# The last stage of a perceiver kernel: raw rows multiplied, mean and deviation put in later, mixing matrices in two alternating chains, half of the mixing on TensorE

## The reference

```
x = x + xattn(layernorm(x), ctx, ...)
x = x + attn(layernorm(x), Wq, Wk, Wv, Wo)
x = x + ffn(layernorm(x), W_res, W_pre, W_post, ...)

# ffn: 4 streams of 256 channels, per token
x_norm = x * rsqrt(mean(x * x) + 1.19e-07)
H_res  = sinkhorn(x_norm @ W_res.T + H_res_base)       # 4 x 4, 50 iterations, tau 0.1
H_pre  = softmax(x_norm @ W_pre.T + H_pre_base)        # 4
H_post = softmax(x_norm @ W_post.T + H_post_base)      # 4
H_res  = (1 - g) * I + g * H_res                       # g = sigmoid(gate)
y      = (sum over n of H_pre[n] * stream n) @ W_branch
out i  = sum over j of H_res[i, j] * stream j  +  H_post[i] * y
```

## Time and profile before

| | us |
|---|---|
| median of 3 runs | 1221.07 |
| lowest and highest run | 1219.29, 1223.58 |
| the profiled execution | 1221.3 |
| span of its trace | 1219.3 |
| PE busy | 1042.8 (86%) |
| DVE busy | 838.3 (69%) |
| ACT busy | 471.3 (39%) |
| POOL busy | 187.7 (15%) |

### The profile page before, as it was taken

How to read it: one execution, slowest core, us unless ns; L and a number is a source line. 1 busy time by engine, 2 the same in 40 slices (tenths; PEclk the granted TensorE clock), 3 DMA queues, 4 the chain that set the end, 5 groups by cost and what they waited for, 6 DMA issues and landing times.

```text
span 1219.3 us, 17027 instructions
## 1 busy us (share of the span) xinstructions
PE 1042.8 (86%) x6208; PEld 872.5 (72%) x6208; DVE 838.3 (69%) x1588; ACT 471.3 (39%) x945; POOL 187.7 (15%) x192
## 2 busy tenths in 40 slices
PE   3999999999999999999999999999989898941100
PEld 2888888888888878888888878888867677741000
DVE  5743437567778778667688766745658997348888
ACT  3422324354455465444454543413232333132300
POOL 0000000233333222332222200000000000127100
PEclk9999999999999999999999999999989999965555
DMA  9785757234443222444443148995470400000001
GB/s 219 150 182 132 168 118 165 66 94 101 102 99 66 64 52 55 99 101 102 102 102 68 31 87 173 215 242 103 87 121 18 63 10 14 1 1 0 0 0 69
DMA packets 161544, 111.07 MB, mean 91 GB/s; under 512 B 73144, under 2 KB 153656, under 8 KB 161488
## 3 DMA queue, kind: packets, MB, share of 16 engines
q1 hardware_dynamic: 160432, 109.29, 41.3%
q10 hardware_dynamic: 1056, 1.05, 0.4%
HBM read 90.91 MB, written 18.87 MB: 90 GB/s over the span
## 4 chain that ended last, share of the span: by engine, by line
PE 75%; DVE 18%; ACT 3%; issue 2%; DMA 1%; SPq 0%; DVEq 0%; POOL 0%; ACTq 0%
PE ps L511 27%; PE ps L457 27%; PE ps L796 7%; PE ps L443 5%; PE ps L522 4%; PE ps L539 3%; DVE xr L1790 2%; DVE wt L1257 2%; DVE small L1762 1%; DVE small L1768 1%; DMA raw<-in_L_xattn_q_proj_w 1%; DVE small L1770 1%; DVE small L1766 1%; DVE small L1773 1%; DVE small L1764 1%
## 5 line engine op out<-in xcount | busy, mean ns | idle before, releaser
L511 PE MATMUL ps<-wt,act 128*128 128x512 f32 x1536 | 389.2, 397 | 0.0
L457 PE MATMUL ps<-wt,act 128*128 128x512 f32 x1440 | 330.8, 392 | 10.8 <-DVE wt L1257 10.8
L457 PEld LDWEIGHTS ps<-wt,act 128*128 128x128 f32 x1440 | 271.1, 189 | 68.5 <-DVE act L1241 7.6
L511 PEld LDWEIGHTS ps<-wt,act 128*128 128x128 f32 x1536 | 276.0, 189 | 49.3
L1257 DVE TENSOR_TENSOR wt<-raw,wt 128x512 fp32r<-128x512 f32 x192 | 120.1, 683 | 86.1 <-ACT wt L899 86.1
L899 ACT ACTIVATE wt<-raw 128x512 fp32r<-128x512 f32 x192 | 106.4, 623 | 97.8 <-PE ps L457 52.1
L1249 DVE STREAM_TRANSPOSE raw<-raw 128x1024 f32<-128x1024 f32 x96 | 112.7, 1218 | 37.3 <-DMA raw<-in_L_xattn_o_proj_w 20.6
L1241 DVE TENSOR_TENSOR act<-ps,act 128x512 fp32r<-128x512 f32 x112 | 75.7, 683 | 86.2 <-ACT act L894 86.2
L1803 POOL TENSOR_TENSOR small<-small 128x4 f32<-128x4 f32 (+2 forms) x64 | 71.3, 1115 | 397.3 <-DVE small L1271 391.4
L796 PE MATMUL ps<-wt,act 128*128 128x512 f32 x480 | 124.7, 412 | 5.6 <-DVE spare L1569 5.1
L894 ACT ACTIVATE act<-ps 128x512 fp32r<-128x512 f32 x112 | 65.9, 596 | 121.9 <-PE ps L443 121.6
(11 more groups left out here) (126 smaller groups left out, 1045.4 us busy)
## 6 DMA issues: line engine op xcount, KB each, us to landing
xr<-in_ctx SPq DMA_DIRECT2D x64, 256.0 KB, 5.8
raw<-in_L_xattn_o_proj_w SPq DMA_DIRECT2D x32, 512.0 KB, 14.3
raw<-in_L_xattn_q_proj_w SPq DMA_DIRECT2D x30, 512.0 KB, 9.2
q_rows<-G SPq DMA_DIRECT2D x64, 128.0 KB, 3.5
xr<-q_rows SPq DMA_DIRECT2D x16, 512.0 KB
ot_hi<-spare SPq DMA_DIRECT2D x64, 128.0 KB, 2.6
act<-ot_hi SPq DMA_DIRECT2D x32, 256.0 KB, 9.4
raw<-in_L_xattn_k_proj_w SPq DMA_DIRECT2D x8, 512.0 KB, 9.6
```

Of the source, the lines that this page charges most:

```text
L457: mm = pe.matmul(banks[t], lhs(p == 2, c, t), wt[:, n_slot, int(p == 1), c, :], start=(acc_from and q == 0), stop=(acc_to and q == 3 * NC ...
L511: mm = pe.matmul(bank, src[int(p == 2)][:, c, kt * P:(kt + 1) * P], wt[:, slot, int(p == 1), c, :], start=(q == 0), stop=(q == 3 * NC - 1))
```

## The change

It touches only what follows the output projection's products (and, ahead of them, where the statistics of a first half are taken).

1. **Raw rows.** PE turns `xr` itself (`turn_rows`): a tile's first half within block 12 + t, its second half within block 13 + t, both at `at_11`; for tile 3 the second half comes after block 15. The product with the 24 weight columns (`logits` on PE) is of raw rows; a product of a matrix of ones with the weights (`s24`) gives the sums by which the mean is taken off. On DVE `logits(t)` is now two instructions: `s24` times minus the mean, added to the product, then times `rz`, plus the base. `rz` now comes from the variance, without ACT's square. The first half's statistics are taken at blocks 9 to 11 and after the loop (`first_stats3`), the rest behind the last add (`last_stats3`). Normalising is ACT's (`normalise_out`, 1024 columns a tile).
2. **Two chains.** Chain 0 is tiles 0 and 1, chain 1 tiles 2 and 3; each works on 32 numbers per partition, with semaphores of its own (`sk_step`, `sk_in`, `sk_out`). Chain 0 runs 4 iterations (`HEAD`) alone, the two then 20 together, an instruction of the one after an instruction of the other; then chain 1 runs 4 alone while ACT serves chain 0, chain 0 runs 4 while ACT serves chain 1, 21 run together, chain 0 finishes, and chain 1 runs its last 4. An epoch is 25 iterations, so there is one new centring instead of four. The first centring has no logarithms any more: the maxima are taken off, and the first row sums are used as factors.
3. **The branch.** ACT makes diagonal matrices (`dmix`, identity times a column of `h8`, 8 of 128 columns a tile). PE sums the four streams by them (`branch`, 8 matmuls of 128 columns), multiplies with `wb` (2 of 256), and puts x + y times `H_post` into PSUM (`base`, 2 of 512 and 4 of 256 columns a tile). For tiles 2 and 3 ACT copies this to `xr`; for tiles 0 and 1 it stays in PSUM.
4. **The mixing.** For tiles 0 and 1 ACT makes 32 diagonal matrices of the mixing factors (`dres`) after `finish(0)`, PE multiplies them with `z` (`mix`, 32 matmuls of 256 columns, each waiting for its matrix) on top of what lies in PSUM, and ACT copies out. Tiles 2 and 3 stay on DVE, 32 instructions as before; tile 3 is stored in two halves.
5. POOL keeps only the roots and a memset of the ones.

The core of the diff:

```diff
-ITERS, EPOCH = 50, 10
+ITERS, EPOCH, HEAD = 50, 25, 4
@@ PE
+                    elif b >= 12:
+                        if b >= 13:
+                            turn_rows(b - 13, 1)
+                        turn_rows(b - 12, 0)
...
                 if b >= 13:
-                    feed(b - 13)
-            feed(3)
+                    logits(b - 13)
+            turn_rows(3, 1)
+            logits(3)
             for t in range(NT):
...
+                branch(t)
+                base(t)
+            for t in range(2):
+                mix(t)
@@ PE, new
+            def mix(t):
+                for half in range(2):
+                    bank = ps[:, base_banks[t][half], :]
+                    for i in (2 * half, 2 * half + 1):
+                        for j in range(NSTR):
+                            pe.wait_ge(d_res, 16 * t + 4 * i + j + 1)
+                            mm = pe.matmul(bank[:, (i % 2) * CW:(i % 2 + 1) * CW], dres[t][:, 4 * i + j, :],
+                                           z[:, t, j * CW:(j + 1) * CW], start=False, stop=(i % 2 == 1 and j == NSTR - 1))
+                    mm.then_inc(mix_done, 1)
@@ ACT
+            exp_chain(1)
+            exp_chain(1)
+            normalise_out(3)
+            sc.wait_ge(h8_in, 1)
+            sc.activation(h8, h8, ACT.Exp).then_inc(h8_out, 1)
+            branch(0)
+            branch(1)
+            log_chain(0)
+            exp_chain(0)
+            log_chain(1)
+            exp_chain(1)
+            branch(2)
+            branch(3)
+            for t in range(2):
+                sc.wait_ge(h_ready, 1)
+                for n in range(16):
+                    sc.activation(dres[t][:, n, :], ident[:], ACT.Copy, scale=hres[:, 16 * t + n:16 * t + n + 1]
+                                  ).then_inc(d_res, 1)
@@ DVE
+            last_stats3(0)
+            last_stats3(1)
+            logits(0)
+            last_stats3(2)
+            logits(1)
+            centre_rows(0)
+            centre_cols(0)
+            last_stats3(3)
+            first_iteration3(0)
+            logits(2)
+            for _ in range(HEAD):
+                iterate((0,))
+            logits(3)
+            centre_rows(1)
...
+            centre_cols(1)
+            first_iteration3(1)
+            joint = EPOCH - 1 - HEAD
+            for k in range(joint):
+                iterate((0, 1), last=0 if k == joint - 1 else None)
...
+            for k in range(HEAD):
+                if k == HEAD // 2:
+                    recentre(0)
+                iterate((1,), last=1 if k == HEAD - 1 else None)
+            for k in range(HEAD):
+                if k == HEAD // 2:
+                    recentre(1)
+                iterate((0,), fresh=0 if k == 0 else None)
+            for k in range(ITERS - EPOCH - HEAD):
+                iterate((0, 1), fresh=1 if k == 0 else None)
+            finish(0)
+            for k in range(HEAD):
+                iterate((1,))
+            finish(1)
@@ SP
+            for t, half, signal, count in ((0, None, mix_out, 2), (2, None, out_ready, 1), (1, None, mix_out, 4),
+                                           (3, 0, out_ready, 2), (3, 1, out_ready, 3)):
```

More of the change, by code:

```diff
@@ L769, in turn_out2, with turn_rows @@
                 tr.then_inc(o2_turned, 1)
[L771 to L781, removed]
+            def turn_rows(t, half):
+                pe.wait_ge(acc_free, (57 if half else 53) + t)
+                if t == 0:
+                    pe.wait_ge(o2_lo, 8)
+                else:
+                    pe.wait_ge(f_ready, 2 * t - 1 + half)
+                for j in range(4):
+                    tr = pe.transpose(ps[:, 6 + half, j * P:(j + 1) * P],
+                                      xr[:, t, (4 * half + j) * P:(4 * half + j + 1) * P], ident[:])
+                tr.then_inc(f_done, 1)
@@ new lines, in base @@
+            def base(t):
+                pe.wait_ge(lg_read, 4)
+                if t == 3:
+                    pe.wait_ge(base_added, 1)
+                for half in range(2):
+                    bank = ps[:, base_banks[t][half], :]
+                    pe.matmul(bank, ident[:], xr[:, t, half * UW:(half + 1) * UW], start=True, stop=False)
+                    if half == 0:
+                        pe.wait_ge(y_read, t + 1)
+                    for i in (2 * half, 2 * half + 1):
+                        mm = pe.matmul(bank[:, (i % 2) * CW:(i % 2 + 1) * CW], dmix[t % 2][:, 4 + i, :], yb,
+                                       start=False, stop=(t >= 2 and i % 2 == 1))
+                mm.then_inc(base_done, 1)
@@ L1212, in _, with copy_rows @@
[L1212 to L1218, removed]
+            sc.activation(gts[:, 1:2], gts[:, 0:1], ACT.Exp, scale=-1.0).then_inc(gate_exp, 1)
+            def copy_rows(t, half):
+                sc.wait_ge(f_done, 2 * t + half + 1)
+                if half == 0 and t >= 2:
+                    sc.wait_ge(lg_done, t - 1)
+                sc.activation(xT[t % 2][:, 4 * half:4 * half + 4, :], four(ps[:, 6 + half, :]), ACT.Copy
+                              ).then_inc(f_ready, 1)
@@ L1221, in _ @@
+            for t in range(2):
+                for half in range(2):
+                    sc.wait_ge(mix_done, 2 * t + half + 1)
+                    sc.activation(xr[:, t, half * UW:(half + 1) * UW], ps[:, base_banks[t][half], :], ACT.Copy
+                                  ).then_inc(mix_out, 1)
         @block.vector
@@ new lines, in invert_cols, with iterate @@
+            def invert_cols(c, last=False):
+                stepped(c)
+                r = v.reciprocal(ub[c], ub[c])
+                if last:
+                    ask(c, r)
+                else:
+                    step(c, r)
+            def iterate(chains, fresh=None, last=None):
+                for c in chains:
+                    if c != fresh:
+                        stepped(c)
+                        step(c, v.tensor_tensor(rows4(of(tk, c)), rows4(of(Kx, c)), over_i(ub[c]), ALU.mult))
+                for c in chains:
+                    if c == fresh:
+                        answered(c)
+                    else:
+                        stepped(c)
+                    step(c, v.tensor_reduce(ua[c], rows3(of(Kx if c == fresh else tk, c)), AX, ALU.add))
+                for c in chains:
+                    stepped(c)
+                    step(c, v.reciprocal(ua[c], ua[c]))
+                scale_rows(chains)
+                for c in chains:
+                    invert_cols(c, c == last)
@@ new lines, in _ @@
+            finish(1)
+            settle()
+            for t, parts in ((2, ((0, 1, 2, 3),)), (3, ((0, 1), (2, 3)))):
+                v.wait_ge(base_added, t - 1)
+                for streams in parts:
+                    for j in range(NSTR):
+                        settle()
+                        for i in streams:
+                            c = 16 * t + 4 * i + j
+                            o = xr[:, t, i * CW:(i + 1) * CW]
+                            done(v.scalar_tensor_tensor(o, z[:, t, j * CW:(j + 1) * CW], hres[:, c:c + 1], o,
+                                                        ALU.mult, ALU.add),
+                                 out_ready if (i, j) == (streams[-1], NSTR - 1) else dv)
```

390 lines of the change are left out of this document (216 added, 174 removed).

## The result

The changed kernel takes 1180.21 us (median of 4 runs, 1178.49 to 1180.74), the kernel before 1221.93 us in the runs beside it (4 runs): ratio 0.9655, 95% interval 0.9638 to 0.9671, faster by 41.7 us. The profiled execution took 1179.86 us, its span is 1178.1. The forecast was 1181.6.

The account below looks back on a forecast made before the run. DVE's path after the last product was taken to bound the tail; its stretches summed to 1176.7, plus 3.1 and 2.0, less 0.2, gave 1181.6 us, 39.5 less than before. Range 1174 to 1196, own case 1174 to 1188 (0.62).

Parts of the forecast that it names:

- The bound: After the last product, the tail is a DVE path, so what happens in it can be priced by DVE's timeline.
- The joint iterations: 41 iterations of both chains on DVE, twelve instructions each: 1.40 us apiece, bounds 1.32 and 1.68.
- the rival in which they don't: DVE instructions don't overlap: a joint iteration takes 2.8 us, +57 us, 1239 in all; chance 0.06.
- both bounds meet: In a joint pair on DVE, issue (2 x 0.11) and the wait within a chain (0.19 + 0.033) both give 0.22 us.
- The rival of slow issue behind a wait: DVE starts behind a wait need 0.14 instead of 0.11: a joint iteration costs 1.68, +11.5 us, 1193; chance 0.13.
- The centrings: Between the joint stretches, one new centring covered by the other chain's four iterations: 12.0 us, to 1126.2, no wait at ACT.
- The last product: PE from block 12 on: the last product ends 1.0 us later, at 1073.4, bounds +0.5 and +2.0.
- The collisions with POOL: DVE's long multiplies in the iterations fall together with POOL's adding and weighing and disappear with them: 5.7 us on L1762.
- half-width instructions and early iterations: The rest of the gain, 8 us: half-width instructions and four of chain 0's iterations run before 1085.5.
- The mixing on PE: After finish(0), from 1156.6: some 4 matmuls at the lower clock, then 28 at 0.48 to 0.55; 17 to 19 us, to 1175.
- The rival of a clock that stays low: PE's clock stays low through the mixing, which lasts 30.7 us to 1187.3; end at 1193; chance 0.17.
- The end: After DVE's mixing at 1176.7: 3.1 us to the span's end and 2.0 outside it, 1181.8, less 0.2 for the median.

Follow-up runs that it names:

- the third chain: The changed kernel with six more vector instructions on 32 numbers in each of the 41 joint iterations, one behind each pair, on data nothing reads: 1193.48 us.
- the added additions: The changed kernel with eight additions of 1024 columns on POOL beside the first joint stretch, on data nothing reads: 1193.88 us.

## Why the prediction was right

**The bound.** The tail was DVE's and still is: the last entries of the chain are its mixing, and what was taken off DVE came off the time (the mixing of two tiles: 13.9 us on DVE, 14.0 in the time).

**The joint iterations** were the largest term: 1.40 forecast, 1.39 measured. The two close pairs of the trace before gave the right answer to whether neighbours overlap, and the rival in which they don't, with the rule of the Trainium skill (VectorE: DVE Perf Modes, "The DRAIN you can't avoid") behind it, is out: the second of a pair starts 0.12 after the first, while that one's record lasts 0.19. What the same section says beside it, that an operation which is not held starts earlier, agrees with this. One step of the working was wrong though it did no harm: "both bounds meet". With the third chain a start takes 0.095 on the mean, so issue asks for 0.19 a pair, and only the wait of 0.23 binds. The rival of slow issue behind a wait (0.14) is out by the same rows.

**The centrings.** 11.0 us (1114.13 to 1125.15) instead of 12.0. One of them on DVE, two additions between chain 1's reciprocal and its next multiply:

```profile
1116.67 0.20 DVE L1884 RECIPROCAL small<-small 128x8 f32<-128x8 f32 x1
1116.79 0.14 DVE L1917 TENSOR_TENSOR small<-small 128x32 f32<-128x32 f32 x1
1116.96 0.19 DVE L1919 TENSOR_TENSOR small<-small 128x32 f32<-128x32 f32 x1
1117.07 0.19 DVE L1895 TENSOR_TENSOR small<-small 128x32 f32<-128x32 f32 x1
```

The multiply starts 0.40 after the reciprocal instead of 0.24, so the additions of one chain cost 0.16 us and not the 0.5 taken: they stand in the other chain's wait. Chain 0's fresh matrix also needs no first multiply, which I had not counted. Chain 1's saves nothing, since chain 0's multiply keeps that turn; the second joint stretch takes 29.2 us, 21 x 1.39. No wait at ACT, as forecast.

**The last product** was the step most off: +1.0 forecast within +0.5 to +2.0, +1.84 measured, and that it lies within the bounds is luck. The sum was about the stretch from the start of block 12 to the last product's end, and this takes 30.8 us (1043.49 to 1074.27) against 31.1 before (1041.34 to 1072.43): -0.3, outside the bounds. The clock gave back its share: it stays at 1.00 there, where block 14 before took 6.9 us instead of 5.5. The work inside was mis-sized: summed by durations it was 9.5 us, from start to start the 28 transposes take 2.7 and the three small products 5.1, 7.8 in all against 7.4 before; on the other side a block that is cut in two takes 5.70 instead of 5.51, 0.7 in the four. What makes the +1.84 is that block 12 starts 2.15 us later (1043.49 against 1041.34), of which 1.0 is there by 907 us, where the code is the same. The other kernels here with this PE code have block 12's start between 1040.8 and 1046.3, each needs 30.8 us from there, and their last products end between 1071.6 and 1077.0. The start moves by itself, by more than the term is worth, and the 1.8 cannot be put down to the change.

**The collisions with POOL** are gone as forecast, and the added additions show that such additions do this. They were worth more than the 5.7 us that the prediction read on L1762, since the other multiply of an iteration had them too:

```profile
L1768 DVE TENSOR_TENSOR small<-small 128x64 f32<-128x64 f32 x49 | 14.1, 289 | 1.7
```

Undisturbed it lasts 0.225, so 49 x 0.064 = 3.1 us more, 9 in all. The forecast doesn't suffer, as its sum has undisturbed durations; its list of the gain's parts does: of the 8 us left there for half-width instructions and early iterations 3 belong to the collisions.

**The mixing on PE** started at the lower clock and got the higher one back after 3.5 us, as taken from the earlier trace rows. Windows of the changed kernel (us, then busy us of PE, PEld, DVE, ACT, POOL, and PEclk):

```profile
1156.00:1159.00 3.00, 3.00 (x8) 2.37 (x8) 2.55 (x14) 3.00 (x12) 0.00 (x0) 0.50 0.00 0
1159.00:1160.00 1.00, 1.00 (x6) 0.81 (x6) 0.86 (x5) 1.00 (x5) 0.00 (x0) 0.94 0.00 0
```

15.8 us in all instead of 17 to 19: at the higher clock a matmul took 0.45 (12.4 us for some 55 records), less than the 0.48 to 0.55 allowed. The rival of a clock that stays low is out for `mix`; the logits of tile 3 did stay low (3.57 us), under cover of chain 0's iterations.

**The end.** Store and rest took 2.5 + 1.8 instead of 3.1 + 2.0. The last store moves half a tile instead of a whole one; no run shows it apart from the rest. The small errors are +0.9 at the last product, -0.6 from there to the first joint pair (11.5 instead of 12.1), -0.3 in the first joint stretch, -1.0 in the centrings, -0.2 in the second joint stretch, +0.2 in DVE's mixing and -0.8 at the end: with rounding the 1.9 us by which the profiled execution (1179.86) is below the 1181.8 of the sum. The median is 0.35 above that execution, where the forecast had taken 0.2 off, which leaves the 1.4 us by which it was too high. So the closeness of the total owes something to errors that cancel.

## What to carry to other kernels

A chain of short dependent vector instructions pays the time until its own result is ready at each step. Two such chains of half the width that take turns fill that time, and the twelve instructions of half width cost less than the six of full width did (1.39 against 1.68 us); the same chains one after the other cost 2.44. Let one chain lead the other by just as many iterations as another engine's answer needs: 2 were better than 4, and 1 brought the waits back (1.6 us) and was no faster. Then look at the end again: with 2 the other engine's share of the mixing came level with DVE's. And keep GpSimd's long additions away from DVE's two-input instructions on the critical path, where each cost 1.7 us.

## What was new about the hardware

- An instruction on VectorE that waits for the one before it starts 0.23 us after it (32 numbers); one that waits for something long done starts 0.12 after it, or 0.095 on the mean when three chains take turns.
- An addition of 1024 columns on GpSimd (2.35 us) stopped exactly one vector multiply (a pair, where two chains run) for up to 1.7 us, and no reduction or reciprocal: beside it they kept 0.29 to 0.32 us a pair.
- The end of the same PE work varied by 5 us among the profiles (1071.6 to 1077.0), and the time of one kernel by 2 to 7 us among its runs, while the stretch from block 12 to that end took 30.8 us in every profile with this PE code. So a stretch should be measured from its own start, and not by where it ends in each of two kernels.
